# Layer 2 of a four-layer graph network on one core: a new order of the engines, and the sum over edges in one pass over high and low halves

## The reference

```
hi = jnp.einsum('bsh,hk->bsk', x, W1[:H])
hj = jnp.einsum('bsh,hk->bsk', x, W1[H:])
h = jax.nn.relu(hi[:, :, None, :] + hj[:, None, :, :] + b1)
y = jnp.einsum('bijk,kl->bijl', h, W2) + b2
y = _layernorm(y, gamma, beta)
out = jnp.einsum('bij,bijh->bih', adj, y)
...
x = _layernorm(x + _L2_gnn_ref(x, adj, ...), axis=-1)
```

## Time and profile before

| What | us |
|---|---|
| median of 3 runs (1710.98 to 1717.81) | 1712.24 |
| time of the profiled execution | 1710.04 |
| its span | 1708.3 |
| layer 2 in it, from the first normalised x to the last sum of squares | 1052.7 to 1582.5 |

### The profile page before, as it was taken

How to read it: one execution, slowest core, us unless ns; L and a number is a source line. 1 busy time by engine, 2 the same in 40 slices (tenths; PEclk the granted TensorE clock), 3 DMA queues, 4 the chain that set the end, 5 groups by cost and what they waited for, 6 DMA issues and landing times. The chain is left out here.

```text
span 1708.3 us, 32251 instructions
## 1 busy us (share of the span) xinstructions
PE 1495.2 (88%) x9961; PEld 1280.6 (75%) x9961; DVE 1247.5 (73%) x2330; ACT 977.0 (57%) x2551; POOL 4.9 (0%) x24
## 2 busy tenths in 40 slices
PE   3664889999999999999999985999999999998655
PEld 2553567778777787777788774999999999997554
DVE  4886667877878777878778853566666666666788
ACT  2564755665556565566656522666666666665554
POOL 0000000000000000000000000000000000000000
PEclk9897889999999999999999998999999999999787
DMA  3220534334433443343334303867667667671122
GB/s 81 63 62 14 213 144 182 153 144 158 175 143 143 161 173 143 143 186 148 143 150 178 145 32 131 314 238 255 247 239 255 243 244 252 241 256 38 56 74 68
DMA packets 100673, 274.61 MB, mean 161 GB/s; under 512 B 8800, under 2 KB 51424, under 8 KB 100576
## 3 DMA queue, kind: packets, MB, share of 16 engines
q1 hardware_dynamic: 100176, 273.52, 43.8%
q10 hardware_dynamic: 400, 0.00, 0.0%
HBM read 143.46 MB, written 130.02 MB: 160 GB/s over the span
## 5 line engine op out<-in xcount | busy, mean ns | idle before, releaser
L827 DVE TENSOR_TENSOR b_vv<-bank,b_vv 128x512 f32<-128x512 f32 (+1 forms) x192 | 113.7, 599 | 156.5 <-ACT b_vv L753 153.1
L1130 DVE TENSOR_REDUCE c_var<-c_ysq 128x4 f32<-128x512 f32 (+1 forms) x192 | 114.0, 594 | 117.0 <-ACT c_ysq L1078 94.4
L722 PE MATMUL bank<-b_wt,b_SIT 128*128 128x136 f32 x1280 | 161.4, 281 | 29.6 <-DVE b_SJ L452 23.2
L657 PE MATMUL wide<-b_vv,put_w 128*128 128x512 f32 (+1 forms) x384 | 171.5, 528 | 11.3 <-DVE b_vv L827 9.4
L722 PEld LDWEIGHTS bank<-b_wt,b_SIT 128*128 128x128 f32 x1280 | 152.8, 190 | 36.9 <-DVE b_SJ L452 23.4
L1020 PE MATMUL wide<-W2c,c_h 128*128 128x128 f32 x1280 | 174.0, 275 | 0.0
L1020 PEld LDWEIGHTS wide<-W2c,c_h 128*128 128x128 f32 x1280 | 169.6, 193 | 4.3
L686 PE MATMUL bank<-b_grs,b_SJ 128*128 128x128 f32 x1280 | 163.9, 286 | 4.2 <-ACT b_os L802 4.2
L686 PEld LDWEIGHTS bank<-b_grs,b_SJ 128*128 128x128 f32 x1280 | 159.6, 201 | 9.3 <-issue 5.1
L1050 PEld LDWEIGHTS bank<-c_z,c_SIT 128*128 128x128 f32 x1280 | 154.4, 194 | 5.5 <-DVE c_z L1138 2.3
L1050 PE MATMUL bank<-c_z,c_SIT 128*128 128x128 f32 x1280 | 155.0, 277 | 2.1 <-DVE c_z L1138 2.1
(11 more groups left out here) (212 smaller groups left out, 3154.9 us busy)
## 6 DMA issues: line engine op xcount, KB each, us to landing
si_d<-b_SI SPq DMA_DIRECT2D x64, 640.0 KB, 3.0
sj_d<-b_SJ SPq DMA_DIRECT2D x64, 640.0 KB, 4.0
sit_d<-b_SIT SPq DMA_DIRECT2D x64, 640.0 KB, 4.9
c_SJ<-sj_d SPq DMA_DIRECT2D x64, 640.0 KB, 4.1
c_SI<-si_d SPq DMA_DIRECT2D x64, 640.0 KB, 5.2
c_SIT<-sit_d SPq DMA_DIRECT2D x64, 640.0 KB, 4.3
xin<-in_x_dram SPq DMA_DIRECT2D x16, 256.0 KB, 3.0
ain<-in_adj_dram SPq DMA_DIRECT2D x16, 256.0 KB, 3.3
```

What stands on the lines that cost most here:

```text
L657: pe.matmul(out, e.put_w[:, pos % Q, :], vv[:, (pos + k) % 2, 0:width(k)], start=(pos % Q == 0), stop=False)
L722: d = pe.matmul(ring[0][:, 0:W], s.SIT[:, ms, j, :], wt[:, (pos - LAG) % 2, j, :], start=(j == 0), stop=(j == TILES - 1))
L827: v.tensor_tensor(vv[:, b, 0:w], bU[b][:, 0:w], vv[:, b, 0:w], ALU.max).then_inc(v_ok, 1)
L1130: v.tensor_reduce(var[:, k, 0:r], ysq[:, k, 0:width(k)].rearrange("p (j f) -> p j f", f=P), AX.X, ALU.add).then_inc(sum_ok, 1)
```

## The change

The order of all three engines in layer 2 is written anew, and the sum over edges takes another form.

- **Sum over edges.** `z` is split as `hi` and `lo` are: ACT writes its high half (`keep_high`, fp32r) and DVE the remainder (`keep_low`) into `zz`, for each chunk. `SIT` is loaded as fp32r. PE then does ten fp32r matmuls of 256 columns, one instruction each, into two banks (`duo`, high and low sums of four graphs). ACT copies the low sums of four graphs out (`rest`), DVE adds the high ones; the multiplication by gamma becomes a separate instruction.
- **Order.** The work of chunk 2 of a graph on ACT and DVE and the splitting of chunks 1 and 2 are done in the next step; gather 0 and rectify 0 of the next graph are done in this one; the sum over edges is of graph n - 2. Gathers use two banks in turn.

For chunks the new names are as before, with the graph as an argument.

```diff
+        s.SIT = sb("SIT", [P, 4, TILES, P], F32R)
         s.xin = sb("xin", [P, 2, P])
...
+        rest = sb("rest", [P, Q, P])
         bb = sb("bb", [P, Q, P])
...
 
         def summed(n, inner):
+            return inner or 2 <= n <= B + 1
+
+        def followed(n, inner):
             return inner or 1 <= n <= B
 
         def part(n, pos, inner, k):
...
                     if N:
                         pe.wait_ge(s.x_ok, g + 1)
                         if inner or g >= 1:
-                            pe.wait_ge(xT_ok, g)
+                            pe.wait_ge(lo_ok, g)
                         pe.transpose(bP[:, 0:P], s.xin[:, (pos + 1) % 2, :], e.ident[:, :]).then_inc(s.xT_mm, 1)
                     if A:
+                        gather(n, pos, 1)
+                    if S:
+                        m, r = n - 2, (pos - 2) % 4
+                        pe.wait_ge(zl_ok, 3 * n - 3)
+                        pe.wait_ge(sit_in[r], 16 * (2 * K + (pos - 2) // 4 + 1))
+                        if r == 0 and (inner or m >= Q):
+                            pe.wait_ge(o_read, batches(K, pos))
+                        for j in range(TILES):
+                            d = pe.matmul(bO[:, r, :, :], s.SIT[:, r, j, :], zz[:, pos % 2, j, :],
+                                          start=(j == 0), stop=(j == TILES - 1))
+                        d.then_inc(o_mm, 1)
+                    if A:
                         mlp(0)
-                        gather(2)
+                    if N:
+                        pe.wait_ge(xT_ok, g + 1)
+                        pe.matmul(bP[:, P:3 * P], xT[:, :], e.W1s[:, :, :], start=True, stop=True).then_inc(p_mm, 1)
+                    if A:
+                        gather(n, pos, 2)
                         mlp(1)
                     if N:
-                        pe.wait_ge(xT_ok, g + 1)
-                        if inner or g >= 1:
-                            pe.wait_ge(lo_ok, g)
-                        pe.matmul(bP[:, P:3 * P], xT[:, :], e.W1s[:, :, :], start=True, stop=True).then_inc(p_mm, 1)
-                    if S:
-                        m, a = n - 1, P * ((pos - 1) % Q)
-                        pe.wait_ge(z_ok, 3 * n)
-                        pe.wait_ge(sit_in[(pos - 1) % 4], 16 * (2 * K + (pos - 1) // 4 + 1))
-                        if (pos - 1) % Q == 0 and (inner or m >= Q):
-                            pe.wait_ge(o_read, batches(K, pos))
-                        for j in range(TILES):
-                            d = pe.matmul(bO[:, a:a + P], s.SIT[:, (pos - 1) % 4, j, :], z[:, (pos - 1) % 2, j, :],
-                                          start=(j == 0), stop=(j == TILES - 1))
-                        d.then_inc(o_mm, 1)
+                        pe.wait_ge(lo_ok, g + 1)
+                        pe.wait_ge(sj_in[(pos + 1) % 4], rounds(K, pos + 1))
+                        pe.wait_ge(si_in[(pos + 1) % 4], rounds(K, pos + 1))
+                        gather(g, pos + 1, 0)
...
+                    def keep_high(n, b, k):
+                        act.wait_ge(z_ok, 3 * n + k + 1)
+                        if inner or n >= 2:
+                            act.wait_ge(o_mm, n - 1)
+                        act.copy(zz[:, b, tiles(k).start:tiles(k).stop, 0:P],
+                                 z[:, b, tiles(k).start:tiles(k).stop, :]).then_inc(zh_ok, 1)
+
+                    F = followed(n, inner)
+                    if F:
+                        square(n - 1, 2)
                     if N:
                         act.wait_ge(s.xT_mm, g + 1)
-                        if inner or g >= 1:
-                            act.wait_ge(p_mm, g)
                         act.copy(xT[:, :], bP[:, 0:P]).then_inc(xT_ok, 1)
-                    if A:
-                        square(0)
-                        rectify(2)
-                        root(0)
-                        square(1)
+                    if F:
+                        keep_high(n - 1, (pos - 1) % 2, 1)
+                    if A:
+                        rectify(n, pos, 1)
+                    if F:
+                        root(n - 1, 2)
+                    if A:
+                        square(n, 0)
                     if N:
                         act.wait_ge(p_mm, g + 1)
                         if inner or g >= 2:
                             act.wait_ge(s.u_mm, 3 * g - 3)
                         act.copy(hi[:, (pos + 1) % 2, :], bP[:, P:3 * P]).then_inc(hi_ok, 1)
-                    if A:
-                        root(1)
+                    if F:
+                        keep_high(n - 1, (pos - 1) % 2, 2)
+                    if A:
+                        rectify(n, pos, 2)
+                        root(n, 0)
+                    if part(n, pos, inner, 1):
+                        act.wait_ge(o_mm, n - 1)
+                        if inner or n > Q + 1:
+                            act.wait_ge(o_read, batches(K, pos) - 1)
+                        act.copy(rest[:, :, :], bO[:, :, 1, :]).then_inc(rest_ok, 1)
...
                     if N2:
                         normalise_x(act, e, s, K, pos + 2, inner or n >= 0)
                     if A:
-                        square(2)
-                        root(2)
+                        square(n, 1)
+                        keep_high(n, pos % 2, 0)
+                    if N:
+                        rectify(g, pos + 1, 0)
+                    if A:
+                        root(n, 1)
 
...
                         v.wait_ge(root_ok, 3 * n + k + 1)
+                        if k == 0 and (inner or n >= 2):
+                            v.wait_ge(zl_ok, 3 * n - 3)
...
+                    def keep_low(n, b, k):
+                        js = slice(tiles(k).start, tiles(k).stop)
+                        v.wait_ge(zh_ok, 3 * n + k + 1)
+                        v.tensor_tensor(zz[:, b, js, P:2 * P], z[:, b, js, :], zz[:, b, js, 0:P].bitcast(F32),
+                                        ALU.subtract).then_inc(zl_ok, 1)
+
...
+                    F = followed(n, inner)
+                    if F:
+                        total(n - 1, 2)
+                        keep_low(n - 1, (pos - 1) % 2, 1)
                     if part(n, pos, inner, 2):
                         q.n = 1
                         q.wait()
                         v.wait_ge(o_read, i + 1)
-                        q.add(v.tensor_tensor(s.res[:, :, :], s.res[:, :, :], bb[:, :, :], ALU.add))
+                        q.add(v.tensor_tensor(s.res[:, :, :], s.res[:, :, :],
+                                              e.gam[:, :].unsqueeze(1).broadcast_to([P, Q, P]), ALU.mult))
...
-                    if A:
-                        if inner or n >= 2:
-                            v.wait_ge(o_mm, n - 1)
-                        total(0)
-                    if A:
-                        scale(0)
-                        total(1)
+                    if F:
+                        scale(n - 1, (pos - 1) % 2, 2)
+                    if A:
+                        total(n, 0)
                     if N:
                         v.wait_ge(hi_ok, g + 1)
                         if inner or g >= 2:
                             v.wait_ge(s.u_mm, 3 * g - 3)
                         v.tensor_tensor(lo[:, (pos + 1) % 2, :], bP[:, P:3 * P], hi[:, (pos + 1) % 2, :].bitcast(F32),
                                         ALU.subtract).then_inc(lo_ok, 1)
-                    if A:
-                        scale(1)
+                    if F:
+                        keep_low(n - 1, (pos - 1) % 2, 2)
+                    if A:
+                        scale(n, pos % 2, 0)
+                    if part(n, pos, inner, 1):
+                        v.wait_ge(rest_ok, i + 1)
+                        if inner or n > Q + 1:
+                            v.wait_ge(s.cen_ok, i)
+                        v.tensor_tensor(s.res[:, :, :], bO[:, :, 0, :], rest[:, :, :], ALU.add).then_inc(o_read, 1)
+                    if A:
+                        total(n, 1)
+                        keep_low(n, pos % 2, 0)
...
                     if part(n, pos, inner, 2):
+                        q.wait()
+                        q.add(v.tensor_tensor(s.res[:, :, :], s.res[:, :, :], bb[:, :, :], ALU.add))
...
                     if A:
-                        total(2)
-                        scale(2)
+                        scale(n, pos % 2, 1)
```

More of the change, by code:

```diff
@@ L947, in layer2_packed @@
         z_ok = sem("z_ok")
+        zh_ok = sem("zh_ok")
+        zl_ok = sem("zl_ok")
+        rest_ok = sem("rest_ok")
         o_mm = sem("o_mm")
@@ L950, in layer2_packed @@
         seq_c = sem("seq_c")
-        bU = e.banks[0:3]
-        bP = e.banks[3]
-        bO = e.banks[4]
+        bU = e.banks[0:2]
+        bP = e.banks[2]
         bY = e.banks[5:8]
+        bO = e.duo[:, :].rearrange("p (q a f) -> p q a f", q=Q, f=P)
         def gathered(n, inner):
@@ L967, in batches, with pair_bank @@
             return 8 // Q * K + pos // Q
+        def pair_bank(pos, k):
```

(22 more changed lines are left out.)

37 lines of the change are left out of this document (15 added, 22 removed).

## The result

The changed kernel takes 1722.93 us in the median beside 1712.38 of before; the ratio is 1.004, 95% interval 1.0021 to 1.006. I had forecast 0.7% faster. The interval lies above 1. The ratio is under the 0.5% that I had called measurable, but the median is over the 1720.8 that I had set for slower. One of the ten runs of the changed kernel, in the slow state, took 4338.53 us at a granted clock of 1.00, for a cause that nothing here shows; it is left out of the ratio, and without it the median is 1722.39. The other nine lie between 1713.6 and 1728.1, those of before between 1710.2 and 1718.5.

The account below looks back on a forecast made before the run. PE bounds layer 2 before, a DVE-ACT chain after: (7.97 - 7.76) x 63 = 13.2 us gained, 2 lost at the ends, 11 us net, so 1700 us, 0.7% faster; forecast 1690 to 1708, range 1660 to 1722.

Parts of the forecast that it names:

- The bound now, and PE after: Layer 2: PE bounds the kernel before at 7.97 us a graph; after the change PE's work is 6.98 us.
- DVE and ACT as the new bound: Layer 2 steps: a chain alternating between DVE and ACT (z, high half, low half) sets the period, 7.76 us a graph.
- The signs that I had named: Layer 2 profile: period near 7.76, PE about 90% busy, DVE over 90%, idling before high-low subtractions and `total(1)`, copies 0.62.
- the one that I had called level with PE: Position 4 of the layer 2 steps: laid out at 6.99 us, beside PE's 6.98.
- with the loop's 0.32 / 8 of before: Layer 2 loop: the jump's cost before, 0.32 us per eight steps, kept, taking the mean from 7.72 to 7.76 us.
- The layer's end: End of layer 2: halves and shorter sum about even, `rest` and gamma 1.4 us more; with the fill 2 us lost.
- PE did not stay the bound: Rival for layer 2: small chain waits leave PE the bound, period 7.1 to 7.2 us, time 1664 or 1654; chance 0.18.
- The no-gain rival: Rival for layer 2: three terms add 0.22 us a graph, period 7.98, time 1715, within 0.5%; chance 0.17.
- The copy at 0.71: No-gain term: ACT's 512-wide copy from SBUF takes 0.71 instead of 0.62 us, adding 0.14 us.
- The wait on two semaphores: No-gain term: such a wait costs 0.12 instead of 0.03 us, 0.09 in positions 1 and 2.
- The dearer jump: No-gain term: a loop restarting three coupled engines may cost twice 0.32 us, adding 0.04.
- The clock did not fall by PE's short waits: Rival for layer 2: PE idling 0.8 of 7.8 us lowers its clock, 1780 at a share of 0.4; chance 0.06.

## Why the prediction was wrong

**The bound now, and PE after.** Right. PE's work was put at 6.98 us a graph; where PE is level with the others the distances are 7.01 in the loop and 6.93 without it. The ten new matmuls take 1.19 us (gather 1 begins its last at 1290.84, the sum 1291.08, mlp 0 at 1292.27).

**DVE and ACT as the new bound.** Right, in mechanism and nearly in size. The four steps came out at 7.23, 8.01, 8.55 and 7.36 for 6.99, 7.96, 8.50 and 7.41, 31.15 for 30.86 in all. The signs that I had named are there, but for one: with the loop of four steps PE is busy 58.69 of 64 us, near the 90% that I gave, and DVE 56.37, 88% and not over 90. The waits of DVE that carry the sum have these rows, and ACT's squares that end two of them these:

```profile
1292.94 0.69 DVE L1179 TENSOR_TENSOR c_zz<-c_z,c_zz 128x512 fp32r<-128x512 f32 x1 [0.36 <-ACT c_zz L1101]
...
1297.56 0.69 DVE L1162 TENSOR_REDUCE c_var<-c_ysq 128x4 f32<-128x512 f32 x1 [0.50 <-ACT c_ysq L1090]
...
1305.50 0.69 DVE L1162 TENSOR_REDUCE c_var<-c_ysq 128x4 f32<-128x512 f32 x1 [0.66 <-ACT c_ysq L1090]
```

```profile
1296.87 0.58 ACT L1090 ACTIVATE c_ysq<-wide 128x512 f32<-128x512 f32 x1
...
1304.81 0.57 ACT L1090 ACTIVATE c_ysq<-wide 128x512 f32<-128x512 f32 x1
```

0.36, 0.50 and 0.66 were laid out as 0.42, 0.50 and 0.62. ACT's new copy, which no row of before showed, takes 0.62 as taken from the earlier trace rows; the subtraction 0.69 for 0.68. The step that is 0.24 too short is the one that I had called level with PE. In it DVE idles 0.19 ahead of `total(0)` for ACT's square, a wait that the layout does not have; written out, this wait is gone and the step takes 6.94.

**The step that failed** is a few words in the sum: "with the loop's 0.32 / 8 of before". The price of a jump was taken over as if it belonged to the loop and not to how its program lies. In place of 0.32 us the jumps cost 6.0 to 6.8 in four cases and 3.0 in one, since ACT stood without its program. That is 27.8 us in all against the 1.6 of five jumps at 0.32; with it the 7.79 us of four measured steps become 8.1 in the mean of 62, longer than the 7.97 of before. Nothing in the timeline of before shows this, but two views that I had at hand bear on it. The page has the packets of the instruction queues, and the order lists show ACT's loop growing. The runs with four steps, with fewer waits, with a shift and without a loop take the jumps away in four ways and land at 1700, 1703, 1704 and 1689, around the 1700 that I had given. That the first is 1700 to the microsecond is luck: in the trace of the changed kernel the end of the layer cost 3.2 more than given and the start and the rest gave 2.3 back, and the kernel before read 1717.5 in that series instead of 1712.

**The layer's end** was put at 2 us and cost 5.2; 1.5 of it came back at the start. The gamma and `rest` cost 1.3 of the 1.4 foreseen (end of the last sum over edges to ACT's last root, 7.12 before, 8.46 after). The rest I had called even, and it was not: the last mlp 2 starts 14.6 us after the last transpose instead of 13.0, and the last sum ends 9.3 us after that mlp 2 starts, not 7.0.

```profile
1577.96 0.28 PE L1029 MATMUL wide<-b2x,ones 128*128 128x256 bf16 x1 [0.81 <-ACT c_h L1083]
...
1584.77 2.50 PE L1049 MATMUL duo<-c_zz,c_SIT 128*128 128x256 f32 x10 [4.90 <-DVE c_zz L1179]
```

Beside the earlier trace rows PE waits 4.90 instead of 2.12 for the last halves, and 2.50 instead of 4.13 for the sum itself do not make up for it; the new sum too runs at a granted clock of 0.5.

**The rivals.** PE did not stay the bound. The no-gain rival, 1715, came near to the time, and two of its three terms are there. The copy at 0.71 is not: it took 0.62. The wait on two semaphores is: the squares end at 1297.45 and 1305.38, and `total(1)` starts 0.11 and 0.12 later, where I had taken 0.03. The dearer jump is too, but for want of a program and not from the coupling of three engines, and at another size, 27.8 / 63 = 0.44 us a graph for the 0.04 that the rival gave it. The clock did not fall by PE's short waits: with the loop of four steps PE is busy 58.69 of 64 us at 1.00. By the rule of the Trainium skill on cycling through banks ("TensorE: Matmul & The Clock Gate", A second HAM failure mode: psum-queue depth-cycling) it would have swung here, and it does not in this trace. Only around ACT's stalls, where PE waits over 4 us in one piece, is the clock lower (0.97 in the stretch above, and right behind one the matmuls of 256 columns start 0.21 us apart instead of 0.12).

The range, 1660 to 1722, left the time out by 0.9 us, for a term that the rival of no gain had at a tenth of its size and from another cause.

## What to carry to other kernels

Before moving or adding instructions in a loop, count what each engine runs in one iteration and look at the packets of the instruction queues in the stretch of the loop: none is the state to keep. When an engine waits for "issue" at the first instruction behind a jump and packets come in each iteration, shorten the iteration, take out redundant waits, move the loop's start or write the loop out before judging the change itself. And laying one period out by hand from start-to-start distances was good to 1% in the mean of four steps; the waits it names are places to put other work, which here brought another 20 us.

## What the runs showed of the hardware that I had not expected

- An ACT loop of 281 instructions cost 6.0 to 6.8 us at four of five jumps, one of 284 only 0.4; moving them by 40 and 27 instructions exchanged the two (1722.9 to 1703.6, and 1733.8 to 1772.7).
- Three added instructions that wait for nothing cost the kernel before 0.19 us a graph, six 0.42, some 0.07 each, in front of `rectify(0)`. Taking 40 waits an iteration out of the changed kernel changed no step outside the jump.
- The same step is 0.17 us longer in a loop than written out in the changed kernel, and equal in the one before. That PE is the bound there is not the reason: the new order with the old sum has PE as its bound too, and takes 8.04 to 8.26 in a loop and 7.92 written out.
- A packet of 8 KB brings about 127 instructions of ACT, waits and register work included (the layer without a loop), and a loop that touched four such pieces was fetched again in each iteration, while those that touched three were not.
